# Local attention in six layers: another hand-written order of steps on four engines, with the small-array products in nine runs per turn where there were twelve

## What is computed

```python
def attn_layer(x, Wqkv, qs, ksc, Wo):          # 16 heads of 64, windows of 32
    qkv = x @ Wqkv
    q, k, v = jnp.split(qkv, 3, -1)
    ...
    q = l2norm(q) * qs
    k = l2norm(k) * ksc
    ...
    q = q * cos * scale + rotate_half(q) * sin * scale
    k = k * cos * inv + rotate_half(k) * sin * inv
    out = local_attention(q, k, v)             # a window of 32 queries sees 64 keys
    ...
    return out @ Wo

for i in range(DEPTH):                          # DEPTH = 6
    x = attn_layer(shift_tokens(x), Wqkv[i], q_scale[i], k_scale[i], Wo[i]) + x
    x = ffn_layer(shift_tokens(x), ln_g[i], ln_b[i], W1[i], b1[i], W2[i], b2[i]) + x
```

## Time and profile before

| what | value |
|---|---|
| median of three runs | 2087.13 us |
| the profiled execution | 2087.44 us, of which the span from first to last instruction is 2085.6 us |
| the stack in it | 109.8 to 1821 us of the span |
| one turn, layer's last (the next one's tables are made in it) | 71.3 us; others 67.2 to 68.6 us |
| PE busy over the span | 91% (DVE 69%, ACT 67%, POOL 69%) |
| mean granted clock of PE | 0.96 of full speed |

### The profile page before, as it was taken

How to read it: one execution, slowest core, us unless ns; L and a number is a source line. 1 busy time by engine, 2 the same in 40 slices (tenths; PEclk the granted TensorE clock), 3 DMA queues, 4 the chain that set the end, 5 groups by cost and what they waited for, 6 DMA issues and landing times. The chain is left out here.

```text
span 2085.6 us, 77661 instructions
## 1 busy us (share of the span) xinstructions
PE 1895.0 (91%) x32069; PEld 1312.6 (63%) x32069; DVE 1446.0 (69%) x2609; ACT 1395.4 (67%) x2781; POOL 1445.9 (69%) x1837
## 2 busy tenths in 40 slices
PE   5648999999999999999999999999999999669958
PEld 4526666666666666666666666666666666456648
DVE  2357687778776877777777867787778786245546
ACT  1157777787777777777777777777787777235425
POOL 1158887888788878887788778877888787112334
PEclk9779999999999999999999999999999999769969
DMA  2011131111311113111113111121111111030002
GB/s 96 0 34 48 48 96 45 46 48 46 95 46 48 46 46 96 48 48 55 40 41 102 55 40 36 41 81 31 30 33 31 30 30 33 2 99 1 18 30 76
DMA packets 67088, 99.85 MB, mean 48 GB/s; under 512 B 15367, under 2 KB 51608, under 8 KB 65970
## 3 DMA queue, kind: packets, MB, share of 16 engines
q1 hardware_dynamic: 65234, 91.72, 15.3%
q0 software_dynamic: 1504, 3.17, 0.4%
HBM read 44.50 MB, written 21.45 MB: 32 GB/s over the span
## 5 line engine op out<-in xcount | busy, mean ns | idle before, releaser
L1074 PE MATMUL b_bank_proj<-layer_weights,b_stream_t 128*128 128x512 f32 x1152 | 589.4, 613 | 34.0 <-DVE b_plain_moved L948 17.9
L948 DVE TENSOR_TENSOR b_plain_moved<-b_bank_proj,b_rope 128x1024 f32<-128x1024 f32 x384 | 464.0, 1219 | 191.8 <-ACT b_squares L834 137.8
L759 POOL TENSOR_TENSOR b_rotated<-b_plain_moved 128x1024 f32<-128x1024 f32 x192 | 453.5, 2362 | 23.1 <-DVE b_plain_moved L948 18.7
L774 POOL TENSOR_TENSOR b_rotated<-b_rotated,b_inv_norm 128x1024 f32<-128x1024 f32 x192 | 365.2, 1902 | 15.6
L834 ACT ACTIVATE b_squares<-b_bank_proj 128x512 f32<-128x512 f32 x384 | 229.1, 597 | 116.1 <-PE b_bank_proj L1074 111.6
L865 ACT ACTIVATE b_k_t<-b_bank_shared 64x512 f32<-64x512 f32 x384 | 226.5, 590 | 119.9 <-PE b_bank_shared L1082 117.4
L1074 PEld LDWEIGHTS b_bank_proj<-layer_weights,b_stream_t 128*128 128x128 f32 x1152 | 186.9, 192 | 136.1 <-issue 45.7
L779 POOL TENSOR_TENSOR b_probs<-b_probs,b_inv_sum 128x512 f32<-128x512 f32 x192 | 200.3, 1044 | 90.1 <-DVE b_inv_sum L969 88.7
L856 ACT ACTIVATE b_q_t<-b_bank_shared 64x512 f32<-64x512 f32 x384 | 225.7, 588 | 34.3 <-PE b_bank_shared L1082 31.4
L1082 PE MATMUL b_bank_shared<-const_tables,b_rotated 128*128 128x128 f32 x1536 | 233.1, 277 | 15.6 <-POOL b_rotated L774 15.2
L1101 PEld LDWEIGHTS b_bank_scores<-b_k_t,b_q_t 128*32 128x32 f32 x12288 | 184.5, 111 | 98.9 <-issue 95.8
(11 more groups left out here) (320 smaller groups left out, 2866.8 us busy)
## 6 DMA issues: line engine op xcount, KB each, us to landing
b_v_shifted<-b_v SPq DMA_DIRECT2D x96, 384.0 KB, 3.5
sorted_rows<-constants SPq DMA_DIRECT2D x135, 129.0 KB, 3.4
layer_weights<-L_ffn_Wqkv SPq DMA_DIRECT2D x6, 1536.0 KB
b_v_shifted<-b_v SPq DMA_DIRECT2D x72, 128.0 KB, 3.4
layer_weights<-L_ffn_w SPq DMA_DIRECT2D x16, 256.0 KB, 5.2
layer_weights<-L_ffn_Wo SPq DMA_DIRECT2D x6, 512.0 KB
c_sorted_in<-sorted_rows SPq DMA_DIRECT2D x23, 129.0 KB, 2.1
layer_weights<-L_ffn_W SPq DMA_DIRECT2D x6, 341.0 KB
```

Of the source, the lines that this page charges most:

```text
L759: nc.gpsimd.tensor_tensor(out=turned[:, k, :], in0=pm[:, k, 0, :], in1=pm[:, k, 1, :], op=ALU.add).then_inc(add_done, 1)
L774: nc.gpsimd.tensor_tensor(out=tk, in0=tk, in1=repeat_last(rn[:, k, :], DH), op=ALU.mult).then_inc(rope_done, 1)
L948: nc.vector.tensor_tensor(to, src.to_broadcast(shape), tab.to_broadcast(shape), ALU.mult).then_inc(mul_done, 1)
L1074: nc.tensor.matmul(out, xs[:, b, t * P:(t + 1) * P], w, start=True, stop=True).then_inc(proj_full, 1)
```

## The change

It puts new lists in place of the four. Each list has the same steps as before (75, 78, 50 and 33 entries, each kind and part as often); their order and their `ahead` numbers differ. No step's own code changes. In `PE_TURN` the three steps "scores (0,0), pv (-1), scores (0,1)" stand side by side as one run, and so do the two scores of tile 1: nine runs. The core of the diff, with what the text ahead speaks of:

```diff
 PE_TURN = [
-    ("scores", -1, 1), ("heads_t", 0, 1), ("project", 1, 0), ("project", 1, 1), ("pv", -2, 0), ("project", 1, 2),
-    ("down", -2, 0), ("heads_t", 0, 2), ("project", 1, 3), ("out", -2, 0), ("heads_t", 0, 3), ("probs_t", -1, 0),
-    ("project", 1, 4), ("project", 1, 5), ("scores", 0, 0), ("probs_t", -1, 1), ("project", 2, 0),
-    ("project", 2, 1), ("pv", -1, 0), ("heads_t", 1, 0), ("project", 2, 2), ("heads_t", 1, 1), ("scores", 0, 1),
-    ("leave", -2, 0), ("project", 2, 3), ("out", -1, 0), ("heads_t", 1, 2), ("heads_t", 1, 3), ("back", -1, 0),
-    ("project", 2, 4), ("project", 2, 5), ("probs_t", 0, 0), ("scores", 1, 0), ("project", 3, 0),
-    ("heads_t", 2, 0), ("project", 3, 1), ("probs_t", 0, 1), ("scores", 1, 1), ("project", 3, 2), ("pv", 0, 0),
-    ("heads_t", 2, 1), ("norm_t", -1, 0), ("project", 3, 3), ("heads_t", 2, 2), ("up", -1, 0), ("heads_t", 2, 3),
-    ("out", 0, 0), ("up", -1, 1), ("enter", 1, 0), ("probs_t", 1, 0), ("scores", 2, 0), ("up", -1, 2),
-    ("up", -1, 3), ("project", 3, 4), ("probs_t", 1, 1), ("project", 3, 5), ("heads_t", 3, 0), ("project", 4, 0),
-    ("project", 4, 1), ("pv", 1, 0), ("heads_t", 3, 1), ("project", 4, 2), ("scores", 2, 1), ("out", 1, 0),
...
+    ("heads_t", 0, 0), ("project", 1, 1), ("pv", -2, 0), ("heads_t", 0, 1), ("project", 1, 2), ("project", 1, 3),
+    ("down", -2, 0), ("heads_t", 0, 2), ("heads_t", 0, 3), ("probs_t", -1, 0), ("project", 1, 4),
+    ("project", 1, 5), ("probs_t", -1, 1), ("project", 2, 0), ("project", 2, 1), ("scores", 0, 0), ("pv", -1, 0),
+    ("scores", 0, 1), ("heads_t", 1, 0), ("project", 2, 2), ("heads_t", 1, 1), ("out", -2, 0), ("heads_t", 1, 2),
+    ("project", 2, 3), ("out", -1, 0), ("project", 2, 4), ("heads_t", 1, 3), ("probs_t", 0, 0), ("back", -1, 0),
+    ("leave", -2, 0), ("project", 2, 5), ("scores", 1, 0), ("scores", 1, 1), ("heads_t", 2, 0), ("project", 3, 0),
+    ("project", 3, 1), ("probs_t", 0, 1), ("heads_t", 2, 1), ("project", 3, 2), ("project", 3, 3), ("pv", 0, 0),
+    ("norm_t", -1, 0), ("heads_t", 2, 2), ("heads_t", 2, 3), ("enter", 1, 0), ("out", 0, 0), ("up", -1, 0),
+    ("scores", 2, 0), ("probs_t", 1, 0), ("up", -1, 1), ("up", -1, 2), ("scores", 2, 1), ("up", -1, 3),
+    ("project", 3, 4), ("heads_t", 3, 0), ("probs_t", 1, 1), ("project", 3, 5), ("project", 4, 0),
+    ("project", 4, 1), ("pv", 1, 0), ("heads_t", 3, 1), ("heads_t", 3, 2), ("project", 4, 2), ("heads_t", 3, 3),
+    ("out", 1, 0), ("probs_t", 2, 0), ("up", -1, 4), ("up", -1, 5), ("scores", 3, 0), ("project", 4, 3),
+    ("probs_t", 2, 1), ("project", 4, 4), ("scores", 3, 1), ("project", 4, 5), ("project", 5, 0),
 ]
 ACT_TURN = [
-    ("probs_t", -1, 0), ("probs_t", -1, 1), ("project", 2, 0), ("project", 2, 1), ("root", 1, 1), ("exp", 0, 0),
-    ("attended", -1, 0), ("attended", -1, 1), ("project", 2, 2), ("heads_t", 1, 0), ("heads_t", 1, 1),
...
+    ("probs_t", -1, 1), ("project", 2, 0), ("root", 1, 1), ("project", 2, 1), ("attended", -1, 0), ("exp", 0, 0),
+    ("attended", -1, 1), ("heads_t", 1, 0), ("heads_t", 1, 1), ("project", 2, 2), ("root", 2, 0), ("exp", 0, 1),
...
 DVE_TURN = [
-    ("residual", 0, 0), ("hidden", -1, 0), ("mul", 4, 0), ("norms", 4, 0), ("share", 2, 0), ("mul", 4, 1),
...
-    ("mul", 7, 1), ("mul", 7, 2), ("scale", 0, 0), ("soft", 5, 1), ("mul", 7, 3), ("share", 5, 1), ("norms", 7, 1),
-    ("soft", 6, 0),
+    ("share", 1, 0), ("scale", -1, 0), ("mul", 3, 2), ("norms", 3, 1), ("mul", 3, 3), ("share", 1, 1),
+    ("soft", 2, 0), ("hidden", -1, 0), ("share", 2, 0), ("residual", 0, 0), ("soft", 2, 1), ("mul", 4, 0),
...
+    ("norms", 6, 1), ("stats", 0, 0), ("soft", 5, 0), ("soft", 5, 1), ("mul", 7, 0), ("mul", 7, 1),
+    ("norms", 7, 0),
 ]
 POOL_TURN = [
-    ("add", -2, 1), ("clamp", -2, 1), ("weigh", -4, 1), ("rstd", -2, 0), ("rope", -2, 1), ("clamp", -1, 0),
-    ("weigh", -3, 0), ("add", -1, 0), ("weigh", -3, 1), ("clamp", -1, 1), ("rope", -1, 0), ("add", -1, 1),
-    ("rope", -1, 1), ("clamp", 0, 0), ("weigh", -2, 0), ("add", 0, 0), ("rope", 0, 0), ("weigh", -2, 1),
...
+    ("add", -2, 1), ("rstd", -2, 0), ("rope", -2, 1), ("clamp", -1, 0), ("add", -1, 0), ("weigh", -3, 0),
+    ("clamp", -1, 1), ("rope", -1, 0), ("weigh", -3, 1), ("add", -1, 1), ("rope", -1, 1), ("clamp", 0, 0),
+    ("weigh", -2, 0), ("add", 0, 0), ("weigh", -2, 1), ("rope", 0, 0), ("add", 0, 1), ("clamp", 0, 1),
+    ("weigh", -1, 0), ("rope", 0, 1), ("weigh", -1, 1), ("clamp", 1, 0), ("add", 1, 0), ("add", 1, 1),
+    ("clamp", 1, 1), ("rope", 1, 0), ("rope", 1, 1), ("clamp", 2, 0), ("weigh", 0, 0), ("add", 2, 0),
...
```

41 lines of the change are left out of this document (18 added, 23 removed).

## The result

| | before | after |
|---|---|---|
| median | 2086.91 us (2084.05 to 2090.17) | 2125.76 us (2120.07 to 2132.76, 4 runs) |
| ratio | 1 | 1.0187 [1.0149, 1.0225] |
| profiled execution, its span | 2087.44, 2085.6 us | 2122.34, 2120.5 us |
| mean granted clock | 0.960 | 0.956 |

What follows compares the result with a forecast made beforehand. PE's own list was taken to bound the kernel (busy 91%). Array shape -10, supply stops +15, layer wait -13 and other waits -3 summed to -11 from 2087.4: 2076 us, range 2054 to 2097.

Steps and rivals of the forecast that it cites:

- the price of the supply stops: PE's stops for instruction blocks of 256 would cost 36 us against 21 before: +15 us, bounds +3 to +37.
- the lead of the queue: How far the queue reads ahead at the border in scores (0,0): 0.8 us there, 0.45 taken in the mean.
- the main stop: Stop in pv (-1) behind a 2.0 us block of small instructions: 1.25 us in 22 turns, 27 us.
- Other waits: Ordinary-turn waits for POOL and DVE, 0.9 for 1.1 us per turn: -3 us (-12 to +20); DMA costs nothing.
- The bound of +37: Upper bound of the supply term, with no lead of the queue anywhere.
- The second stops: Further short blocks behind pv (1) in turns 10 to 14 and scores (0,1) in turns 19 to 23: 9 us.
- the layer's wait: PE's wait for POOL's table at a layer's end shrinks and the clock holds: -13 us (-19 to -3).
- supply costs more: Rival: no queue lead at the border in scores (0,0), supply 58 us instead of 36, 2098; decides from 1.8; chance 0.17.
- The array's shape: Three runs fewer of another array shape save a net 0.4 us per turn over 24 turns: -10 us (-3 to -13).
- the borders can be counted through the list: Block borders every 256 instructions: pv (-1) stops near instruction 183 in turn 13, 6 earlier each turn.
- every turn from 1 to 23: The block of 256 small instructions, 2.0 us, lies wholly inside the new run in each of these turns.
- calls fetching hidden: Skill's rule, set among the rivals: stops are no supply and vanish with the old neighbours, 2040; chance 0.03.

Runs made afterwards that it cites:

- the run made in the kernel before: Kernel before, only PE's list changed so that scores (0,0) and (0,1) stand directly beside pv (-1,0): 2164.79 us, 1.0386.
- opening the run: Kernel after, whole-array steps parting scores (0,0), pv (-1,0), scores (0,1): 2178.51 us with residual moved two places; 2084.76 us with ACT and DVE orders following.
- the filler: Two useless 512-column products ahead of pv (-1,0) in every turn: in the kernel after 2131.46 us, in the kernel before 2121.86 us.
- an opened order: Kernel after with small steps parted, queues following, scores (1,1) behind project (3,1): 2044.24 us; with 64 small products once ahead of the first turn, 2063.78 us.

## Why the prediction was wrong

The step that failed is the price of the supply stops: +15 for a true +44. Inside it, the lead of the queue at the main stop was taken from a stretch without copies, while "Other waits" said of the copies that DMA costs nothing here.

- **The lead.** The main stop was 3.7 - 2.0 less a lead of 0.45, that is 1.25; it measured 2.08. The lead was read from one stretch, and right for it: the traced border is at 1039.83, the packet at 1040.12. The new order brings the same border among SP's copies of v, and there I find no lead: the packet starts 1.0 to 2.3 us after PE has crossed the border in turns 2 to 22. With no lead and 3.7 the stop is 1.7; the distance from border to border is 4.02 us in the mean of these turns, 1.53 to the packet's start, 1.12 for the packet and 1.37 until PE goes on. With the 0.65 to the packet's start that the kernel before has at this border it would be 3.1 and the stop 1.2, close to the 1.25 forecast. So by estimate some 18 of the 19 us (0.88 in 21 turns) are the packet's late start among the copies. That the copies cause it fits the traces of both kernels and of the run made in the kernel before, but no run tested it. The bound of +37, with no lead, was too low for the same reason. Together +19 in 22 turns (45.7 for 27).
- **The second stops.** 9 us were counted, in turns 10 to 14 and 19 to 23; 20.0 measured. pv (1,0) stops in turns 14 to 20, and scores (1,1) in turns 2 to 4, the first of which my count had shorter and the second not at all. Half of the 20.0 us stand behind blocks of 4.2 to 7.9 us of work, longer than the 3.7 that the count asked for; there the packet was late. +11.
- **The clock.** Eleven of the stops have the clock at its lower level at them for 3.4 or 6.8 us; no term had it, though the text had just that effect at the layer's wait. The rest grew by 12.3 us while the layer's own part of it went away.
- The rival "supply costs more" had the mechanism and its place right, and the stop is past its deciding 1.8, but its 2098 left out the second and third point, and its chance of 0.17 was too low. The range ended short of it.

What was right:

- The array's shape: -14.3 us in 23 turns, 0.6 per turn, a little more than was given (-10, to -13). The change of shape inside the run is nearly free, and so opening the run gave back 10.2 us.
- That the borders can be counted through the list: instruction 182 for 183, and 6 earlier each turn from turn 3 to 22. Between turns 2 and 3 it is 12 and between 22 and 23 it is 40, where `enter` ends and `leave` begins. In turn 23 the block before the stop in pv (-1,0) is no longer inside the run, as "every turn from 1 to 23" had it. The old stops in scores (2,1) are gone, those in pv (0,0) small.
- The layer's wait: the layer turn 7 is 1.1 us longer than the next for 4.0, with the clock at 1.00, and project (4,2) waits 2.3 us in all for 11.9. (Turns 3 and 15 are longer for the stops and the low clock in them.)
- Other waits, -3 forecast: heads_t (2,2) has lost its 12.4 us as written, and project (3,2) waits for mul (3,0) as written, but 0.7 a turn (16.0 us), with colder products behind it 1.1, where 0.6 was said. With the layers' 9.7 all waits together give -1.6.
- The Trainium skill, Runtime: NRT & Kernel Launch, Instruction fetch mechanics, calls fetching hidden. The packets agree with its blocks of 256 instructions; the 2.08 us per turn, and the filler that fits into them, do not agree with its being hidden where the products are this small. The same section has the cost of crossing a block's border as mostly hidden, which holds for most of the ten borders of a turn here: 41 stops in 23 turns.

The last column of the table is only partly settled: I didn't separate the low clock from the other slower products behind a gap in a run of its own, and no run holds the clock up with the stops in place. Open too are what the packet would do without the copies, and why some packets start up to 12 us after the border. That an opened order loses nothing elsewhere is shown for this position of the borders and, with 23.4 us of stops, for one other.

## What to carry to other kernels

Where an engine takes small instructions (here two per 16 ns product), the length of PE's work between two borders of 256 instructions is a resource like a buffer: count the borders through the list, and let no block be shorter than some 4 us. That is needed but not enough: where transfers run as the packet is due, or the packet is late for a reason not found here, small products stop behind longer blocks too. Small steps should be parted by wide products, even if each run then costs some 0.2 us for its two changes of array shape, and an edit of PE's order must bring the other queues with it: the largest losses here, 93 and 104 us, came with waits that my own moves made.

A change that moves by a few us should be tried at more than one position of the borders: 64 extra products ahead of everything, a change that does nothing, cost 15 us in one kernel and 15 to 20 in another.
